# Low parts behind high ones: GpSimd's order, TensorE's waits and the place of the second state's setting

## What is computed

```python
x = x + linear_attention(layernorm(x))   # 16 heads of 16; softplus features, running sum over tokens
x = x + ffn(layernorm(x))                # gated recurrence over the batch axis, c -> f*c + i*g
x = x + softmax_attention(layernorm(x))  # 16 heads, ALiBi, causal
x = x + ffn(layernorm(x))

def step(c, xt):                         # the recurrence of ffn: xt is one batch, c the state
    ft = sigmoid(xt @ wf.T + c @ uf.T + bf)
    it = sigmoid(xt @ wi.T + c @ ui.T + bi)
    gt = tanh(xt @ wc.T + c @ uc.T + bc)
    return ft * c + it * gt
h = tanh(einsum('tbi,oi->tbo', x, wo) + c_final @ uo.T + bo)
```

## Time and profile before

| | |
|---|---|
| median of 3 runs | 2726.83 us (2723.98 to 2726.88) |
| the profiled execution's own time | 2732.81 us |
| its span, first to last instruction | 2730.7 us |
| TensorE busy | 2267.1 us (83%) |
| VectorE busy | 1702.9 us (62%) |
| ScalarE busy | 1261.3 us (46%) |
| GpSimd busy | 783.0 us (29%) |
| mean granted TensorE clock | 0.923 |

### The profile page before, as it was taken

How to read it: one execution, slowest core, us unless ns; L and a number is a source line. 1 busy time by engine, 2 the same in 40 slices (tenths; PEclk the granted TensorE clock), 3 DMA queues, 4 the chain that set the end, 5 groups by cost and what they waited for, 6 DMA issues and landing times.

```text
span 2730.7 us, 57194 instructions
## 1 busy us (share of the span) xinstructions
PE 2267.1 (83%) x24094; PEld 1196.8 (44%) x24195; DVE 1702.9 (62%) x3805; ACT 1261.3 (46%) x2025; POOL 783.0 (29%) x658
## 2 busy tenths in 40 slices
PE   3568887988889766488899999999999989998964
PEld 1346555665556543223244443443444434433332
DVE  5647566565654544367677676776777767667327
ACT  2323434343342212135565655666656655655623
POOL 2224232323311111523143243351533513202110
PEclk9789999999999978679899999999999999999977
DMA  2101010010100111321122122230321201202053
GB/s 83 47 17 48 32 48 32 32 48 19 45 17 32 48 47 47 106 79 59 64 93 87 48 85 66 68 111 24 102 78 63 80 30 64 70 26 96 27 216 123
DMA packets 127439, 171.33 MB, mean 63 GB/s; under 512 B 8864, under 2 KB 94880, under 8 KB 127184
## 3 DMA queue, kind: packets, MB, share of 16 engines
q1 hardware_dynamic: 123088, 167.15, 18.3%
q10 hardware_dynamic: 4096, 0.53, 0.1%
HBM read 91.11 MB, written 76.02 MB: 61 GB/s over the span
## 4 chain that ended last, share of the span: by engine, by line
PE 64%; DVE 17%; ACT 7%; issue 4%; DMA 3%; ACTq 3%; SPq 2%; POOL 1%; DVEq 0%; POOLq 0%
PE general L885 10%; PE general L562 9%; PE out_of_heads L763 9%; PE scores L704 6%; PE scores L680 4%; PE general L896 4%; PE general L548 4%; DVE maxima L1399 3%; PE turned_scores L718 3%; ACTq L1104 3%; PE general L528 3%; PE out_of_heads L636 2%; DMA k_stacks<-k_stack 2%; PE out_of_heads L646 2%; PE scores L594 2%
## 5 line engine op out<-in xcount | busy, mean ns | idle before, releaser
L1399 DVE TENSOR_REDUCE maxima<-scores 128x1 f32<-128x512 f32 (+3 forms) x1536 | 798.0, 553 | 392.5 <-PE scores L680 241.7
L1083 ACT ACTIVATE probs_turned<-turned_scores 128x512 f32<-128x512 f32 x1152 | 682.8, 600 | 531.5 <-PE turned_scores L680 282.8
L704 PE MATMUL scores<-k_stacks,q_stacks 51*128 51x512 bf16 (+3 forms) x1536 | 455.0, 341 | 74.5 <-DVE maxima L1399 47.9
L718 PE MATMUL turned_scores<-q_stacks,k_stacks 53*128 53x512 bf16 (+3 forms) x1536 | 446.2, 334 | 39.7 <-ACT probs_turned L1083 39.6
L704 PEld LDWEIGHTS scores<-k_stacks,q_stacks 51*128 51x128 bf16 x1536 | 125.7, 95 | 325.3 <-DVE maxima L1399 196.1
L680 PE MATMUL scores<-mask_scores,identity 64*128 64x256 bf16 (+3 forms) x954 | 250.8, 263 | 0.0
L680 PE MATMUL turned_scores<-mask_turned,identity 64*128 64x128 bf16 (+3 forms) x969 | 249.8, 258 | 0.0
L1704 POOL TENSOR_TENSOR ln_low<-ln 128x512 bf16<-128x512 f32 x128 | 138.5, 1089 | 283.1 <-DVE ln L1381 283.1
L1683 POOL TENSOR_SCALAR ln<-x_for_attention,ln_mean_var,ln_rstd 128x256 f32<-128x256 f32 x104 | 128.2, 1243 | 209.1 <-DVEq L1478 119.3
L1621 POOL TENSOR_TENSOR state_low<-state_doubled,state_high 128x2048 bf16<-128x2048 f32 x14 | 57.0, 4072 | 380.6 <-ACT state_high L1016 380.6
L680 PEld LDWEIGHTS scores<-mask_scores,identity 64*128 64x128 bf16 (+1 forms) x954 | 90.5, 95 | 165.9 <-issue 85.5
(11 more groups left out here) (231 smaller groups left out, 5171.5 us busy)
## 6 DMA issues: line engine op xcount, KB each, us to landing
x_after_attention<-x_residual SPq DMA_DIRECT2D x16, 1024.0 KB, 5.2
x_times_wo<-x_wo_out SPq DMA_DIRECT2D x64, 256.0 KB, 2.2
k_stacks<-k_stack SPq DMA_DIRECT2D x64, 212.0 KB
q_stacks<-q_stack SPq DMA_DIRECT2D x64, 204.0 KB
x_for_attention<-in_x SPq DMA_DIRECT2D x8, 1024.0 KB, 5.3
x_residual<-in_x SPq DMA_DIRECT2D x8, 1024.0 KB, 5.3
x_for_attention<-x_after_attention SPq DMA_DIRECT2D x8, 1024.0 KB, 12.1
ffn_h<-x_times_wo SPq DMA_DIRECT2D x32, 256.0 KB, 6.9
```

Of the source, the lines that this page charges most:

```text
L704: mx = pe.matmul(bank_s[:, first * P:(first + tiles) * P], QS[at:at + QROWS, r, i * P:(i + 1) * P], KS[at:at + QROWS, r, k0 * P:(k0 + tile ...
L718: ex = pe.matmul(bank_t[:, first * P:(first + tiles) * P], KS[at:at + KROWS, r, j * P:(j + 1) * P], QS[at:at + KROWS, r, i0 * P:(i0 + tile ...
L1083: nc.scalar.activation(PR[:, s % SLOTS, :], TB[s % 2][:, :], ACT.Exp).then_inc(sem["ex_taken"], 1)
L1399: r = dve.tensor_reduce(MP[:, gg % 2, g, at:at + 1], max_bank[m][:, first * P:(first + tiles) * P], AX.X, ALU.max)
```

## The change

It moves and relaxes; no compute instruction is added or taken out. On GpSimd, phase 1's state_low of a batch goes from the end of a round into the next one, behind chunks_low of the second half and behind the first split_q. On TensorE, the high parts of LN output (both phases) and of phase 1's attention output wait for the numbers themselves (ln_norm, o_taken1) instead of their low parts, and the wait for low parts stands before the low turns. On VectorE, take_chunk of a batch's first chunk (from the second batch on) waits for the low parts of the batch before, since TensorE's wait no longer guards that buffer; and set_state of phase 2 goes from before the statistics of phase 2's first LN to behind its normalising (step 78 of stage -2).

```diff
@@ tensor, fill
-                        if k == 1:
-                            pe.wait_ge(sem[f"ln_low{phase}"], 4 * norms_to(phase, "ln1", nb))
+                        if k in (1, 3):
+                            pe.wait_ge(sem[f"{('ln_norm', 'ln_low')[part]}{phase}"], 4 * norms_to(phase, "ln1", nb))
...
-                        if k == 13:
-                            pe.wait_ge(sem[f"o_low{phase}"], 2 * (pb + 1))
+                        if k in (13, 15):
+                            pe.wait_ge(sem[("o_taken1", "o_low1")[part]], (NT, 2)[part] * (pb + 1))
...
-                        if k == 54:
-                            pe.wait_ge(sem[f"ln_low{phase}"], 4 * norms_to(phase, "ln2", pb))
+                        if k in (54, 56):
+                            pe.wait_ge(sem[f"{('ln_norm', 'ln_low')[part]}{phase}"], 4 * norms_to(phase, "ln2", pb))
@@ tensor, turns (phase 2)
-                    if k == 0:
-                        pe.wait_ge(sem["ln_low2"], 4 * norms_to(2, "ln1", b + 1))
+                    pe.wait_ge(sem[("ln_norm2", "ln_low2")[k // 2]], 4 * norms_to(2, "ln1", b + 1))
...
-                    if k == 56:
-                        pe.wait_ge(sem["ln_low2"], 4 * norms_to(2, "ln2", b - 1))
+                    pe.wait_ge(sem[("ln_norm2", "ln_low2")[k // 2 - 28]], 4 * norms_to(2, "ln2", b - 1))
@@ vector
             def take_chunk(n):
+                if n and n % NT == 0:
+                    dve.wait_ge(sem["o_low1"], 2 * (n // NT))
...
                         for c in range(4):
                             normalise(0, XA, c, 2)
+                    if k == 78 and fb == 0:
+                        set_state()
...
             last_state_low(1, 1)
             state_part(1)
-            set_state()
@@ gpsimd
                 if batch_in(nb):
                     split_q(nb, 0)
+                if batch_in(pb - 1):
+                    state_low(1, pb - 1)
                 if batch_in(pb):
                     layer_norm(1, 2, XR, pb)
...
-                if batch_in(pb) and pb < B - 1:
-                    state_low(1, pb)
```

## The result

The median of 6 runs is **2749.16 us** (2747.10 to 2753.40), beside 2726.86 us for the kernel before in the same session: a ratio of 1.0071, 95% interval 1.0056 to 1.0086, 22 us slower. The forecast was 2740 us. The profiled execution took 2750.24 us, with a span of 2748.4 us: 17.7 more than before's 2730.7, at the same mean clock of 0.923. The traces account for these 17.7; the rest of the 22 is that before's profiled execution was 6 us above its median and the changed kernel's 1 us above its own.

The account below looks back on a forecast made before the run. TensorE was 64% of the chain, with VectorE's gates and phi on it without slack. Gains of 15.8 us against losses of 11.6, 14.3 and 4 gave +14 us: forecast 2740 us, range 2717 to 2753.

Parts of the forecast that it names:

- rivals 2 and 3: VectorE only slowed beside GpSimd, 2715 us, chance 0.13; one collision missed or hidden, 2722 to 2725 us, chance 0.11.
- (A): First LN: only the second half of the low turn moves, a gain of 0.9 us.
- (G): Ends of stages 1 to 7: attention_out_low's second half delays VectorE's gates, a loss of 7 x 1.65 = 11.6 us.
- (H): Stages 2 to 6: state_low delays VectorE's second phi, a loss of 5 x 2.85 = 14.3 us.
- (I): TensorE's clock: longer waits behind phi may bring 1.2 GHz, a loss of 4 us, bounds 0 and 20.
- rival 4: TensorE's clock falls at most of the twelve new waits: 2753 to 2760 us, chance 0.06.
- (B): Stage 7's start: TensorE's wait for the attention output's low part goes, a gain of 4.0 us.
- (C): Stage 8's start: high turn no longer waits, low turn waits for ScalarE's copy, a gain of 7.1 us.
- (E): Phase 2's entry: moved set_state lets the LN end sooner but precedes VectorE's high copy, a gain of 2.7 us.
- (F): Phase 2's last second LN: the high turn goes one piece sooner, a gain of 1.1 us.
- (D): Phase 1's last second LN: VectorE copies its half at the same time as before, 0.
- (J): VectorE's new wait before a batch's first take_chunk has 15 us to spare and costs 0.

Follow-up runs that it names:

- E1: The changed kernel with GpSimd's second chunks_low also waiting for the stage's last gates and state_low directly behind it, ahead of split_q: 2705.26 us, ratio 0.9930.
- E2: The changed kernel with state_low directly behind chunks_low, ahead of split_q; chunks_low still starts beside the gates: 2727.70 us, ratio 1.0007.
- E5: E1 with 14 VectorE instructions on a scratch buffer (2.8 us) ahead of the second phi in stages 2 to 6: 2731.77 us, ratio 1.0013.
- E10: E1 with 7 VectorE instructions on a scratch buffer (1.4 us) ahead of the second phi in stages 2 to 6: 2726.02 us, ratio 0.9990.
- E3: The changed kernel with chunks_low waiting for the stage's last gates; state_low still behind split_q: 2726.34 us, ratio 1.0000.
- E9: The kernel before with only set_state moved behind phase 2's first normalising: 2729.19 us, ratio 0.9998.
- E6: The changed kernel with state_low and chunks_low each as four GpSimd instructions of a quarter, in the same places: 2727.78 us, ratio 1.0002.
- E12: E1's kernel measured again, on one other chip: 2709.39 us, ratio 0.9932.

## Why the prediction was right, and by how much it missed

The sign, the place and the mechanism were right: the rivals 2 and 3 (only slowed, or one collision) fall with L1376 at 3.48 us and L1239 at 2.38, and E1 shows that nothing else lost. By the traces the forecast was +14 and the result +17.7; by the medians +14 and +22. That the traces come so close is partly luck: stages 2 to 6 grew by 34.3 us, 6.9 each, where the terms for them give 22.5 + 4 and the forecast's own sign was 4 to 6 each; some 5 us that fell the other way before stage 1's end, and are not the change's (A below), hide most of that.

- **(G)**: forecast 1.65 us at seven stage ends; measured 2.38 - 0.68 = 1.70, seven times: 11.9.
- **(H)**: forecast 2.85 us in five stages; measured 3.48 - 0.68 = 2.8: 14. The rule for it had a gap: in before's trace no residual add lies beside state_low, only beside split_q's tensor_scalar. The changed kernel's row of 447.21 shows what the forecast took for granted.
- **(I), the term that was mis-sized.** Forecast 4 us, bounds 0 to 20. G and H put 5 x (1.70 + 2.80) = 22.5 us of delay into stages 2 to 6; the stages grew by 34.3. The rest, 12, goes with 30.7 us more low clock in them (85.3 - 54.6), half of which is 15.4, so that not all of the half was lost here. The step that failed was "I take half of five": it gave a clock loss to some of the waits behind phi and none to the gates. The trace shows one at every phi, and a longer stretch at nearly every stage's start. E2 shows 17.1 us of low clock for the gates alone, and E5 and E10 show that a plain stall brings it, in full even at 1.4 us. The result lies in the forecast's own range of 2733 to 2752, on rival 4's side.
- **(A)**: forecast 0.9. VectorE's copy of the low half starts at 32.98 instead of 33.90: 0.9. Yet the last attention output of stage 1 is taken 6.0 us sooner (297.41 instead of 303.41). The other 5.1 are low clock that fell otherwise before stage 1's end, 64.9 us instead of 75.1, and half the difference is 5.1. Two runs show that it is not the change's: E3 has the changed kernel's instructions up to there, had 75.1 us, and took that output only 1.0 us sooner than before; E9 has before's instructions, had 64.9 us, and took it at 297.72, 5.7 us sooner.
- **(B)**: forecast 4.0, measured 3.5 in E1 (99.4 to 95.9) but 0.7 after. There the last gates of stage 7 were 1.7 us late, and low clock in the stage rose from 10.2 to 18.5 us. The forecast had charged the 1.7 to G. E9's stage 7, with before's instructions, took 102.2 us, so this term is known to some 3 us only.
- **(C)**: forecast 7.1, measured 7.2 in E1 (65.7 to 58.5), 8.2 after. The changed kernel's rows at stage 8's start:

```profile
1015.03 1.90 ACT L1014 CAST state_high<-state_doubled 128x2048 bf16<-128x2048 f32 x1 [4.32 <-DVE state_doubled L1241]
1016.83 1.00 ACT L1074 COPY ln_turned_high<-general 128x1024 bf16<-128x1024 bf16 x1
1017.00 4.06 POOL L1622 TENSOR_TENSOR state_low<-state_doubled,state_high 128x2048 bf16<-128x2048 f32 x1 [3.28 <-ACT state_high L1014]
...
1017.98 1.86 PE L528 MATMUL general<-identity,attention_out_low 128*128 128x128 bf16 x16 [5.48 <-ACT ln_turned_high L1074]
```

The low turn starts 2.95 us behind state_high's start, where it had been 10.08, and its releaser is ScalarE's copy behind state_high, as forecast.

- **(E)**: forecast 2.7. The changed kernel's entry into phase 2, beside the earlier trace rows:

```profile
1107.14 4.83 DVE L1381 TENSOR_SCALAR ln<-x_for_attention,ln_mean_var,ln_rstd 128x256 f32<-128x256 f32 x8
1112.35 1.76 DVE L1324 MEMSET state_doubled<- 128x2048 f32 x1 [0.37 <-issue]
...
1116.86 2.29 DVE L1329 TENSOR_TENSOR state_low<-state_doubled,state_high 128x2048 bf16<-128x2048 f32 x1
1119.07 0.68 DVE L1337 COPY ln_turned_high<-general 128x1024 bf16<-128x1024 bf16 x1
1120.88 0.69 DVE L1337 COPY ln_turned_low<-general 128x1024 bf16<-128x1024 bf16 x1 [1.13 <-PE general L528]
```

Set_state takes 6.8 us, 1112.35 to 1119.15, as forecast, and the copy of the high half stands right behind it, so 2.8 are gained in E1 and E9. Counted from phase 1's last state_high, the changed kernel itself gained 1.6 up to the low copy, since its last state parts came 1.2 us later, 8.0 instead of 6.8 us behind state_high.
- **(F)**: forecast 1.1; the copies of the turned halves come 1.0 us sooner against the end of the last second LN, but from that end to the end of the span it is 96.06 us instead of 96.14: 0.1 gained. TensorE starts its next products 1.0 us sooner too (5.03 instead of 6.07 us behind the LN's end). Some 0.4 goes in low clock before the first ScalarE copy behind them (10.18 instead of 10.84), and most of what is left in the last such copy, which now waits for a DMA. The forecast stopped at TensorE's start and did not ask what releases the tail:

```profile
2667.55 0.59 ACT L1134 COPY x_wo_out<-general 128x512 f32<-128x512 f32 x1 [0.47 <-DMA x_times_wo<-x_wo_out]
```

- **(D), (J)**: 0, as forecast; VectorE's waits show none for the low attention output.

The Trainium skill, page "SBUF — State Buffer", section "Who interferes with whom", says that the engine that issues first keeps the shared ports for its whole instruction and that the other blocks altogether. For GpSimd's tensor_tensors these traces agree: both stopped rows end 0.54 us behind GpSimd's, and E6 shows the hold pass on at the end of each piece. For its tensor_scalar they don't: before's two split_q instructions ran from 69.82 to 75.49, yet L1376, begun at 73.08, ended at 74.30, and L1377 behind it, with two SBUF inputs, took the 1.23 us that it takes alone. There the measurement decides: beside that instruction L1376 is slowed from 0.68 to 1.22 us, and not stopped.

```profile
69.82 5.67 POOL L1654 TENSOR_SCALAR probs_turned<-qk_block,mask_even_odd 128x1024 f32<-128x1024 f32 x2 [6.94 <-DVE qk_block L1377]
...
74.33 1.23 DVE L1377 TENSOR_TENSOR q_stacks<-qk_block,ffn_h 128x1024 f32<-128x1024 f32 x1
```

## What to carry to other kernels

An engine with 1% of the chain can set its length: when an instruction of GpSimd is moved, list what VectorE runs in its new window, and which of those rows have all inputs in SBUF. Here one added wait, and state_low moved ahead of split_q, turned +22 us into -20. Where an overlap can't be avoided, shorter pieces can help: they gave back 21 of these 44 us. And where TensorE already waits near its limit, price a new stall as itself plus the low clock behind it: 1.4 and 2.8 us a stage cost 3.4 and 4.6 here (0.5 less each if E12 is taken for the kernel without a stall).

## What was not expected of the hardware

- A stall of VectorE of 1.4 us brought as much low clock of TensorE (20.5 us in five stages) as one of 2.8 us (17.1 us), by one profile of each. The two profiles of the kernel without a stall, E1 and E12, differ by 6.8 us of low clock in these stages.
- The spread between executions goes with TensorE's clock, not with work. E1 and E12 are one kernel: the profiled spans are 2692.9 and 2706.0 us, with 341.9 and 382.8 us of low clock, and 6.0 of the 13.1 us between them lie in phase 1. In phase 2 the same holds between kernels that have the same instructions there: from phase 1's last state_high to the end the changed kernel took 1657.5 us with 226.1 us of low clock, and E1 1640.6 us with 181.5. So in one profile each, a part of the change is read to some 3 us in stages 2 to 6 and to some 6 us over phase 1.
